# Final normalisation stage: centring on ScalarE, scaling and residual addition in one VectorE operation

## The reference

```python
x = x + _layernorm(attention(_layernorm(x)))
x = x + _layernorm(experts(_layernorm(x)))        # the last line ends in the stage of this study

def _layernorm(x, axis=-1, eps=1e-05):
    m = jnp.mean(x, axis=axis, keepdims=True)
    v = jnp.var(x, axis=axis, keepdims=True)
    return (x - m) / jnp.sqrt(v + eps)
```

## Time and profile before

| | us |
|---|---|
| median of 3 runs | 963.0 |
| the profiled execution, its own time | 962.78 |
| its span, from the first to the last instruction | 961.0 |
| PE busy over the span | 822.5 (86%) |
| DVE busy | 661.5 (69%) |
| ACT busy | 364.8 (38%) |
| POOL busy | 116.7 (12%) |

### The profile page before, as it was taken

How to read it: one execution, slowest core, us unless ns; L and a number is a source line. 1 busy time by engine, 2 the same in 40 slices (tenths; PEclk the granted TensorE clock), 3 DMA queues, 4 the chain that set the end, 5 groups by cost and what they waited for, 6 DMA issues and landing times. The chain is left out here.

```text
span 961.0 us, 30663 instructions
## 1 busy us (share of the span) xinstructions
PE 822.5 (86%) x13456; PEld 629.2 (65%) x13456; DVE 661.5 (69%) x1220; ACT 364.8 (38%) x683; POOL 116.7 (12%) x173
## 2 busy tenths in 40 slices
PE   6794779789999999999999787998779999999910
PEld 5683665676777777687687464666566887788800
DVE  2799699799789789879877988787691222222238
ACT  2605334435534644544554451332321222222215
POOL 2000000000000000000000000000002454544345
PEclk9895988999999999999999987998889999999965
DMA  8301004300101021020020020020176999999376
GB/s 307 72 23 47 3 3 168 108 3 25 62 18 39 3 69 27 24 70 23 4 69 24 3 70 23 2 89 2 48 286 220 362 362 346 344 360 358 96 266 278
DMA packets 49632, 113.09 MB, mean 118 GB/s; under 512 B 8688, under 2 KB 8816, under 8 KB 49504
## 3 DMA queue, kind: packets, MB, share of 16 engines
q1 hardware_dynamic: 44384, 100.70, 29.1%
q0 software_dynamic: 5120, 10.49, 4.8%
HBM read 84.34 MB, written 26.84 MB: 116 GB/s over the span
## 5 line engine op out<-in xcount | busy, mean ns | idle before, releaser
L468 PE MATMUL bank<-xnT,wring 128*128 128x256 f32 x768 | 183.6, 396 | 2.1 <-ACTq L681 1.3
L468 PEld LDWEIGHTS bank<-xnT,wring 128*128 128x128 f32 x768 | 149.3, 198 | 24.9 <-ACTq L681 1.5
L587 PE MATMUL bank<-late,ffn_w 128*128 128x256 f32 x480 | 117.3, 394 | 0.0
L1754 DVE TENSOR_TENSOR hid<-ps_g,sg 128x160 f32<-128x160 f32 x32 | 10.4, 324 | 148.5 <-ACT sg L1650 148.5
L942 DVE SCALAR_TENSOR_TENSOR cv<-pre,taps,cv 128x1024 f32<-128x1024 f32 x72 | 92.4, 1283 | 18.1 <-ACTq L707 14.4
L587 PEld LDWEIGHTS bank<-late,ffn_w 128*128 128x128 f32 x480 | 90.8, 195 | 15.2 <-issue 1.1
L1509 POOL MEMSET xgT<- 128x512 f32 x2 | 1.0, 532 | 686.9 <-POOLq L1834 686.9
L1609 PEld LDWEIGHTS ps_g<-xgT,wring 128*128 128x128 f32 x640 | 74.4, 192 | 10.9 <-issue 10.9
L1609 PE MATMUL ps_g<-xgT,wring 128*128 128x128 f32 x640 | 74.8, 275 | 1.3 <-ACT xgT L1640 1.3
L1640 ACT ACTIVATE xgT<-ps_x 128x320 f32<-128x320 f32 x32 | 14.0, 437 | 132.8 <-PE ps_x L1598 132.8
L549 PE MATMUL bank<-wo,o_ch 128*128 128x512 f32 x128 | 60.1, 605 | 0.6 <-DVE o_ch L1086 0.6
(11 more groups left out here) (202 smaller groups left out, 1474.2 us busy)
## 6 DMA issues: line engine op xcount, KB each, us to landing
wring<-in_ffn_W_gate SPq DMA_DIRECT2D x20, 512.0 KB, 7.6
wring<-in_ffn_W_up SPq DMA_DIRECT2D x20, 512.0 KB, 9.6
wring<-in_ffn_W_down SPq DMA_DIRECT2D x20, 512.0 KB, 10.7
x_in<-in_attn_x SPq DMA_DIRECT2D x8, 512.0 KB, 3.7
x_res<-in_attn_x SPq DMA_DIRECT2D x8, 512.0 KB, 4.8
side_rows<-late SPq DMA_DIRECT2D x8, 512.0 KB, 7.0
x_rows<-x SPq DMA_DIRECT2D x8, 512.0 KB, 3.2
h_rows<-h SPq DMA_DIRECT2D x8, 512.0 KB, 4.4
```

The costliest lines, as they stand in the source:

```text
L468: m = te.matmul(bank[:, c * COLS:(c + 1) * COLS], wqkv[:, w, kt, ct * P:(ct + 1) * P], xnT[:, kt, :], start=(kt == 0), stop=(kt == KT - 1))
L587: m = te.matmul(bank[:, c * COLS:(c + 1) * COLS], w[:, kt, ft * P:(ft + 1) * P], hT[:, kt, :], start=(kt == 0), stop=(kt == KT - 1))
```

## The change

ACT no longer multiplies. For each tile, ACT writes z_shift = -mean with a Copy activation on 128x2, takes Ln of the variance, waits for both, centres each row with an Identity activation that has the bias alone, and then takes Exp for z_rs, which now signals z_norm. B(n) is gone from DVE. A(n) becomes two scalar_tensor_tensor on 128x512, one for each b: tile x z_rs + r_all, with z_rs as a scalar for each partition. A(n) now comes two loop steps after M(n), not three: DVE runs M0, M1, M2, A0, M3, A1 up to M7, A5, A6, A7. For tiles 4 to 7 ACT first waits until A of the tile four before is done, since its buffers are written again. Two semaphores are gone.

```diff
-        def z_inverse(r, q):
+        def z_centre(r, q):
             act.wait_ge(z_stats, ZQ * r + q + 1)
+            if r > 0:
+                act.wait_ge(z_first, ZQ * (r - 1) + q + 1)
+            sc_e.activation(z_shift[q][:, :], z_mv[q][:, :, 0], ACT.Copy, scale=-1.0).then_inc(act_chain, 1)
             sc_e.activation(z_rs[q][:, :], z_mv[q][:, :, 1], ACT.Ln, bias=eps[:, 0:1]).then_inc(act_chain, 1)
-            act.wait_ge(act_chain, 1)
+            act.wait_ge(act_chain, 2)
             act.sem_clear(act_chain)
-            sc_e.activation(z_rs[q][:, :], z_rs[q][:, :], ACT.Exp, scale=-0.5).then_inc(z_rstd, 1)
-
-        def z_scale(r, q):
-            act.wait_ge(z_shifts, ZQ * r + q + 1)
             for b in range(B):
-                last = sc_e.activation(tile_in[ZQ * r + q][:, b, :], tile_in[ZQ * r + q][:, b, :], ACT.Identity, bias=z_shift[q][:, b:b + 1], scale=z_rs[q][:, b:b + 1])
-            last.then_inc(z_norm, 1)
+                tile = tile_in[ZQ * r + q][:, b, :]
+                sc_e.activation(tile, tile, ACT.Identity, bias=z_shift[q][:, b:b + 1])
+            sc_e.activation(z_rs[q][:, :], z_rs[q][:, :], ACT.Exp, scale=-0.5).then_inc(z_norm, 1)
 
         for n in range(STEPS):
-            z_inverse(n // ZQ, n % ZQ)
-            if n > 0:
-                z_scale((n - 1) // ZQ, (n - 1) % ZQ)
-        z_scale(ZR - 1, ZQ - 1)
+            z_centre(n // ZQ, n % ZQ)
...
-        def z_bias(r, q):
-
-            dve.wait_ge(z_rstd, ZQ * r + q + 1)
-            v.scalar_tensor_tensor(out=z_shift[q][:, :], in0=z_mv[q][:, :, 0], scalar=-1.0, in1=z_rs[q][:, :], op0=ALU.mult, op1=ALU.mult).then_inc(z_shifts, 1)
-
         def z_add(r, q):
             n = ZQ * r + q
             dve.wait_ge(z_norm, n + 1)
             dve.wait_ge(r_in, 16 * SLOTS)
-            v.tensor_tensor(tile_in[n], tile_in[n], r_all[:, 2 * n:2 * n + 2, :], ALU.add).then_inc(z_first, 1)
-
-        for n in range(STEPS + 3):
+            for b in range(B):
+                last = v.scalar_tensor_tensor(out=tile_in[n][:, b, :], in0=tile_in[n][:, b, :], scalar=z_rs[q][:, b:b + 1], in1=r_all[:, 2 * n + b, :], op0=ALU.mult, op1=ALU.add)
+            last.then_inc(z_first, 1)
+
+        for n in range(STEPS + 2):
             if n < STEPS:
                 z_moments(n // ZQ, n % ZQ)
-            if 1 <= n <= STEPS:
-                z_bias((n - 1) // ZQ, (n - 1) % ZQ)
-            if n >= 3:
-                z_add((n - 3) // ZQ, (n - 3) % ZQ)
+            if n >= 2:
+                z_add((n - 2) // ZQ, (n - 2) % ZQ)
```

More of the change, by code:

```diff
@@ L1421, in expert_part @@
     z_stats = sem("z_stats")
-    z_rstd = sem("z_rstd")
-    z_shifts = sem("z_shifts")
     z_norm = sem("z_norm")
```

## The result

The changed kernel takes 966.8 us (median of 15 runs, 963.72 to 969.11), against 962.24 us for the kernel before in the same comparison (15 runs, 957.74 to 965.33). The ratio is 1.0044, with a 95% interval of 1.0028 to 1.0061: slower, by 2.7 to 5.9 us. The forecast was 966.3 us.

The account below looks back on a forecast made before the run. PE carries the span, but the change touches only the last 33.3 us, bounded by GpSimd's joins, then VectorE. With joins between halves the last add moves from 957.67 to 960.93 us, +3.3 us: median 966.3 us, range 961.5 to 967.9.

Parts of the forecast that it names:

- The exclusion: Last 33.3 us: a GpSimd join and a VectorE instruction with two SBUF inputs block each other for a whole instruction.
- The order between the halves: Between an add's two halves on VectorE, a waiting GpSimd join goes first: +3.3 us, chance 0.50.
- The argument from the pipe: VectorE's next instruction starts only when the pipe is empty, leaving the shared port pair free between an add's halves.
- The steps of the sum: Joins and adds timed in turn through the final stage: last add ends at 960.93 us, now 957.67, +3.3 us.
- The unseen operations: Instructions not in the old trace: VectorE half add 684 to 742 ns, taken as 742; ScalarE Identity some 714 ns.
- more than 742 ns: Sign of failure: the prediction fails if one half of a VectorE add costs more than this.
- ACT as cover: ScalarE's chain from moments to z_norm, 2.0 to 2.1 us, is hidden for tile 7 by two VectorE adds (2.64 us).
- The new wait on z_first: ScalarE's wait costs nothing, since the add of the tile four before ends before this tile's moments start.
- The halves stay together: Rival: VectorE keeps the port between an add's halves, no join enters; +0.3 us, 963.3 us, chance 0.37.
- No exclusion: Rival: the new add form doesn't exclude a GpSimd join, so VectorE never waits; -2.9 us, 960.1 us, chance 0.06.

Follow-up runs that it names:

- PSUM version: Changed kernel, but ScalarE writes the centred halves to PSUM and VectorE's scale-and-adds read them there; 958.43 us, ratio 0.9966 to the kernel before, stage 26.8 us.
- split add in the kernel before: Kernel before, with only the residual add on 128x1024 cut into two adds on 128x512; 966.16 us, ratio 1.0029, stage 33.6 us.
- one-add run: Changed kernel, but each pair of scale-and-adds is one 128x1024 tensor add, without the multiplication; 962.11 us, ratio 0.9989 to the kernel before.
- quarter-add kernel: Changed kernel, with each scale-and-add as four instructions on 128x256 instead of two on 128x512; 970.19 us, ratio 1.0083 to the kernel before.
- split joins: Changed kernel, with each GpSimd join as two instructions on 128x512; 965.35 us, ratio 1.0026 to the kernel before, stage 32.5 us.
- two POOL adds: Changed kernel with adds reading PSUM, but GpSimd does the residual adds of tiles 4 and 6; 960.06 us, ratio 0.9961 to the kernel before.

## Why the prediction was right

*The exclusion and its price.* The exclusion was read from B; the PSUM version, where neither engine waits, confirms it.

*The order between the halves.* This was the open step, to which the prediction gave 0.50 against 0.37 for the rival, and it decided the sign. The changed trace and the split add in the kernel before settle it for the forecast. The one boundary in the trace of before at which DVE went on, B3 to A1, would have spoken for the rival; the prediction rightly counted it as no evidence, since POOL was not yet waiting. (The last section shows joins that won a boundary though they were no earlier, so what decides such a close case is open.) By its own chances it put 0.35 on a slowdown of more than 2.9 us, which came, and 0.60 on a time within 2.9 us of before. So the likeliest mechanism came true, but the prediction didn't hold it for much likelier than its rival.

*The argument from the pipe.* The prediction's sentence on the empty pipe gives only half of what the Trainium skill says there (VectorE: DVE Perf Modes, section "The DRAIN you can't avoid"): the section adds that a next instruction that is not held starts earlier. The records here overlap by 0.07 to 0.08 us, which fits that addition. So the page gave no reason to expect the pair free between the halves; the runs show it.

*The steps of the sum.* The stage began 0.91 us earlier than in the trace of before. With that shift the forecast puts the end of tile 0's first half at 937.32 us, P4 at 939.52, the second half at 940.07, P5 at 942.27, tile 1's halves at 942.82 and 945.57, P7 at 947.77 and the last add at 960.02. Measured: 937.32, 939.52, 940.08, 942.28, 942.82, 945.58, 947.78 and 959.97.

*The unseen operations.* The line's own view gives the half add's median as 744 ns (742 taken from L942's 58 ns pointer price on 684, so the sign "more than 742 ns" was set too close; 2 ns on 16 halves is 0.03 us), and the Identity as 714 ns, the value taken.

```profile
L1786 DVE SCALAR_TENSOR_TENSOR wring<-wring,z_rs,r_all x12: 718/744/2828, 935.7 to 956.6; 128x512 f32<-128x512 f32 x12
```

```profile
L1681 ACT ACTIVATE wring<-wring,z_shift x12: 705/714/722, 931.2 to 951.6; 128x512 f32<-128x512 f32 x12
```

*ACT as cover.* From the end of M7 at 956.02 us to the end of Exp at 957.99 it took 1.97 us (2.0 to 2.1 forecast), and the last add followed A6 at 958.6 us with no wait. The new wait on z_first cost nothing, as forecast.

*What the stage leaves out.* The medians differ by 4.6 us, the stages by 3.2. The interval of the ratio (2.7 to 5.9 us) holds both; nothing in the two traces before 921 us points to a further 1.4 us, and I take it as scatter, which no run here proves. That the whole time came within 0.5 us of the forecast is thus partly luck: the forecast added 3.3 us to 963.0, while the median of the kernel before came out at 962.24 in 15 runs and the loss at 4.6 us. The lower end of the range, 961.5, is also 0.2 us below what its own working gives (963.3 less 1.6), which changes nothing here.

*The rivals.* "The halves stay together" (963.3 us) was worked out with the same rows, and the one-add run bears its mechanism out: 29.1 us, and 8 x 0.19 us more for pointers and second start-ups, make a stage of 30.6 us as an estimate, where the rival's sum had 30.3. "No exclusion" was wrong for the changed kernel, but its number, 2.9 us under before, is what the PSUM version gives when the exclusion is really taken away (3.2 in the stage).

## What to carry to other kernels

Where GpSimd runs long SBUF instructions beside VectorE, count a VectorE instruction with two SBUF inputs as one that can wait, and count its boundaries: as long as GpSimd has work ready, an instruction cut in two let one GpSimd instruction in between here, at its full length. Fusing a multiply into the add saved VectorE nothing here, since the per-partition scalar forced two instructions where one had done. If one input can lie in PSUM, as here by letting ScalarE write there, the wait goes altogether: that version ran 0.34% under the kernel before (0.16 to 0.52%).

## What the runs showed of the hardware that I had not expected

At a VectorE boundary a join won even when it was no earlier. In the quarter-add kernel the second quarter's record begins at 938.32 us and P4's at 938.33 (2.34 us long, so it did not wait at all), and the quarter waited:

```profile
938.32 2.64 DVE L1788 SCALAR_TENSOR_TENSOR wring<-wring,z_rs,r_all 128x256 f32<-128x256 f32 x1
938.33 2.34 POOL L1549 TENSOR_TENSOR wring<-wring 128x1024 f32<-128x1024 f32 x1 [0.22 <-DMA wring<-side_rows]
```

The other two boundaries of this add are alike, and both times the join goes first, again 2.34 us long:

```profile
940.88 2.62 DVE L1788 SCALAR_TENSOR_TENSOR wring<-wring,z_rs,r_all 128x256 f32<-128x256 f32 x1
940.88 2.34 POOL L1549 TENSOR_TENSOR wring<-wring 128x1024 f32<-128x1024 f32 x1 [0.21 <-DMA wring<-side_rows]
...
943.42 2.65 DVE L1788 SCALAR_TENSOR_TENSOR wring<-wring,z_rs,r_all 128x256 f32<-128x256 f32 x1
943.45 2.34 POOL L1549 TENSOR_TENSOR late<-late,wring 128x1024 f32<-128x1024 f32 x1 [0.23 <-DMA late<-side_rows]
```

In the kernel before, A1's record began 0.02 us ahead of P6's, and A1 went first. The difference may be that P6 follows another join without a pause, whereas P4 came fresh; no run here separates these. As far as these rows show, it bears on a boundary only when both engines arrive within some hundredths of a microsecond. The second surprise is how well a stage can be worked out from one trace: from the first join to the last add the forecast held to 0.05 us, and the stages expected for six of the eight further kernels within 0.3 us, while whole times of one kernel, with ten runs or more, spread over 5 to 11 us. Of the other two, the split joins gained 0.8 us where at least 1 was expected, and the two POOL adds missed by 1.3 us.
